# Eleven normalised x pieces turned by DMA transposes instead of by TensorE between products

## The chip, the cores and the metric

The kernel runs on one core of one Trainium2 chip. The metric is the device time of one execution in microseconds (us). Three runs of the kernel before gave 1950.42, 1950.77 and 1952.95 us; the median, 1950.77, is the time before.

## The reference

Eight sequences of 256 tokens and 1024 features pass through cross-attention and a feed-forward block, each with a layer norm ahead of it and a residual behind it:

```
x = x + xattn(layernorm(x), ctx, Wq, bq, Wk, bk)
x = x + ffn(layernorm(x), gate, up, down)

xattn: Q = text @ Wq.T + bq;  K = ctx @ Wk.T + bk
       softmax(Q @ K.T / 32) @ ctx
ffn:   g = x @ Wg.T;  u = x @ Wu.T          (Wg, Wu: 3584 x 1024)
       (silu(g) * u) @ Wd.T                 (Wd: 1024 x 3584)
```

The three feed-forward weights come as 4-bit codes (one int32 each) with a scale for each block of 64, and are decoded in the kernel. Inputs and output are f32.

## The kernel before, in words

**Number format.** Every operand of a large product is split into a high and a low f16 part; a product is three matmuls (high by high, high by low, low by high), so an x form is a pair of f16 tiles.

**Stages.** `prepare` makes the attention matrix and the statistics. `attend` works through the eight batches; `step(b)` on each engine has ten phases. In step b the residual of batch b-1 is added (`residual`), its moments are taken (`moments`), and y of batch b-2 is normalised (`y_normalise`). `feed_forward` follows: 28 stages of seven products by two sides (`slot`), one side being four batches (1024 tokens in f16 forms), and then the down products. ScalarE (ACT) and VectorE (DVE) decode weights all the while, in fixed numbers of steps per phase (`streams.act.run`, `streams.dve.run`), and the SP queue turns the decoded pieces with DMA transposes (`turn_piece`, L301).

**The seven x forms.** The feed-forward products are a seven-product scheme, so a normalised batch gives seven forms j = 0..6 (`t_rows`): three are rows of y (0, 3, 5), four are sums that GpSimd (POOL) makes (`t_sum`; 1, 2, 4, 6). Each form must lie transposed in `T[side][j]` before product j of stage 0 uses it.

**Two ways to turn a form.** The early way (batches 0 to 4, and j = 0, 1, 2 of batch 5; 38 pieces): `t_hi` on ACT and `t_lo` on DVE write the f16 pair into a ring of four slots `t16` (T_RING = 4; `t_hi` waits until the piece four numbers earlier has been turned), `t_turn` on SP issues a DMA transpose into a second ring, `t_store` on SP stores it to the DRAM buffer `keep_x`, and POOL loads all of a form for a side at once (`t_load`, L1254; 1 MB for side 0, 256 or 512 KB for side 1). The late way (`LATE`, 18 pieces: j = 3, 5, 4, 6 of batch 5 and all of batches 6 and 7): `late_turn` issues four 128x128 f32 transposes on TensorE (PE) into a PSUM bank, `late_hi` (ACT, L1273) and `late_lo` (DVE, L1280) write the f16 pair from the bank straight to its place. Late turns 0 to 3 lie in the last attention step, 4 to 17 ahead of the products of stage 0, their number by product written out by hand:

```
then.product(pe, 0); turn_probs(LAST); attended(LAST, 0..3)
m = 4
for k, count in enumerate((2, 2, 2, 1, 0, 2, 2, 1, 1, 1), 1):
    for _ in range(count): ...; late_turn(nc, pe, t, m); m += 1
    then.product(pe, k)
```

**Order around the change.** All engines run in program order. In stage 0, product k is form k of side 0 for k = 0..6 and form k-7 of side 1 for k = 7..13. Product k of side 0 waits for the load `T[0][k]`; on side 1 for the load `T[1][k-7]` and for the late forms. In the handover POOL's order is: the loads of side 0 (j = 0, then 1 to 6), the loads (1, 3), (1, 4), (1, 5), (1, 6), the four sums of batch 6, the loads (1, 0), (1, 1), (1, 2), the four sums of batch 7. `copied` (ACT) and `combined` (DVE) move products between PSUM banks: product 4 waits for `combined(2)`, which DVE runs behind `scales(7)`. The SP queue stores y of batch 6, the last two pieces, y of batch 7 (`store_y`, L1369), and then turns weights. Loads by POOL are on DMA queue q0, everything from SP on q1; both use the same 16 DMA engines.

## Time and profile before

| | before |
|---|---|
| median of three runs | 1950.77 us |
| the profiled execution's own time | 1948.33 us |
| its span, first to last instruction | 1946.5 us |
| PE busy | 1909.0 us (98%) |
| DVE busy | 1621.4 us (83%) |
| ACT busy | 1454.8 us (75%) |
| SP queue and POOL queue, share of the 16 DMA engines | 38.5%, 24.3% |

The span is that of one profiled execution; 1.8 us of its time lie around the span. A group of instructions is named by line, engine, operation and tile. Times in views by time are us from the start of the span. The handover from attention to feed-forward, where the change lies, is at 370 to 440 us.

### The profile page before, as it was taken

The numbers are of one execution on the slowest core, as the hardware profiler recorded it, in microseconds if no ns is written. First come the engines' busy times: TensorE is split into PE (matmuls) and PEld (weight loads), VectorE is DVE, ScalarE is ACT, GpSimd is POOL, SyncE is SP. The second block draws the span as 40 slices with busy tenths as digits, with TensorE's granted clock in tenths as the row PEclk, the third lists the DMA queues.
The fourth block names the chain that finished last, engine by engine and source line by source line (L and its number), as shares of the span: only waits on it lengthen the run. The fifth ranks groups of instructions, "written<-read, shape, count | busy, mean of one in ns | idle before, by whom it ended". The sixth has DMA issues, their size and how long they took to land.

```text
span 1946.5 us, 29468 instructions
## 1 busy us (share of the span) xinstructions
PE 1909.0 (98%) x9758; PEld 969.8 (50%) x9758; DVE 1621.4 (83%) x2671; ACT 1454.8 (75%) x2710; POOL 372.7 (19%) x570
## 2 busy tenths in 40 slices
PE   8989999989999999999999999999999999999999
PEld 3468888744444444444444444444444444444444
DVE  6758899977898898898898898898798888896963
ACT  3867768567989988988988988988999999900000
POOL 0011434431121121121121121121132222200010
PEclk9999999999999999999999999999999999999999
DMA  9123999964555555455455455455488999983462
GB/s 350 31 71 93 211 296 271 270 238 107 130 141 125 125 143 124 127 148 125 121 145 130 121 140 136 119 139 133 115 209 228 242 223 202 246 255 131 161 229 85
DMA packets 427416, 323.00 MB, mean 166 GB/s; under 512 B 361088, under 2 KB 361088, under 8 KB 425344
## 3 DMA queue, kind: packets, MB, share of 16 engines
q1 hardware_dynamic: 381152, 167.47, 38.5%
q0 software_dynamic: 44032, 153.65, 24.3%
q8 instruction: 77, 1.26, 0.3%
q14 instruction: 75, 0.61, 0.1%
q10 hardware_dynamic: 2080, 0.01, 0.1%
HBM read 154.31 MB, written 82.31 MB: 122 GB/s over the span
## 4 chain that ended last, share of the span: by engine, by line
PE 57%; ACT 19%; DVE 8%; issue 7%; DMA 2%; SPq 1%; POOL 1%; DVEq 0%; ACTq 0%; POOLq 0%
PE ps L2108 35%; PE ps L2150 12%; PE ps L1524 7%; ACT sq L346 7%; ACT sq L342 5%; ACT w L346 2%; DVE w L362 2%; ACT w L342 2%; PE ps L1559 1%; PE ps L1497 1%; DVE tail L2260 1%; ACT halves L414 1%; ACT tail L2181 1%; DVE halves L430 1%; ACT tail L2196 1%
## 5 line engine op out<-in xcount | busy, mean ns | idle before, releaser
L2108 PE MATMUL ps<-T,wS 128*128 128x512 f16 x4704 | 1017.6, 379 | 4.3 <-DVE ps L2215 2.7
L2108 PEld LDWEIGHTS ps<-T,wS 128*128 128x128 f16 x4704 | 459.8, 98 | 558.6 <-issue 5.1
L346 ACT ACTIVATE sq<-sq 128x512 f32<-128x512 f32 x898 | 520.0, 635 | 0.0
L362 DVE SCALAR_TENSOR_TENSOR w<-sq,w 128x512 f32<-128x512 f32 x590 | 417.5, 708 | 115.3 <-ACT sq L346 105.5
L342 ACT ACTIVATE sq<-q 128x512 f32<-128x512 int32 x598 | 366.3, 640 | 50.9 <-DVE w L362 46.5
L2150 PE MATMUL ps<-T,tail 128*128 128x512 f16 x1584 | 345.0, 379 | 5.5 <-issue 2.4
L2150 PEld LDWEIGHTS ps<-T,tail 128*128 128x128 f16 x1584 | 154.6, 98 | 193.6 <-issue 5.1
L1524 PE MATMUL ps<-T 128*128 128x256 f16 x1536 | 171.3, 273 | 1.9 <-DVE T L1740 1.9
L2150 PE MATMUL ps<-T,wS 128*128 128x512 f16 x768 | 168.7, 379 | 3.6 <-DMA wS<-keep_h 2.5
L430 DVE SCALAR_TENSOR_TENSOR halves<-w,halves 128x512 f16<-128x512 f32 x240 | 163.9, 692 | 6.8 <-ACT halves L414 6.4
L2056 POOL DMA_DIRECT2D keep_h<-tail x196 | 106.7, 545 | 296.1 <-DVE tail L2260 292.3
L1524 PEld LDWEIGHTS ps<-T 128*128 128x128 f16 x1536 | 150.2, 98 | 19.3 <-DVE T L1740 2.1
L414 ACT CAST halves<-w 128x512 f16<-128x512 f32 x204 | 127.5, 626 | 40.8 <-DVE w L362 31.5
L2260 DVE SCALAR_TENSOR_TENSOR tail<-tail 128x512 f16<-128x512 f32 x196 | 134.1, 684 | 10.6 <-ACT tail L2196 10.5
L2196 ACT CAST tail<-tail 128x512 f16<-128x512 f32 x196 | 120.6, 616 | 5.4 <-DVE tail L2229 5.4
L2150 PEld LDWEIGHTS ps<-T,wS 128*128 128x128 f16 x768 | 74.6, 98 | 95.4 <-issue 4.2
L284 POOL DMA_DIRECT2D q<-in_L_ffn_up_q x52 | 28.1, 540 | 353.5 <-DVE w L362 257.3
L1428 POOL TENSOR_TENSOR T<-tail,T 128x256 f16<-128x256 f32 x64 | 58.7, 917 | 188.5 <-ACT T L1646 188.5
L287 POOL DMA_DIRECT2D q<-in_L_ffn_down_q x56 | 42.9, 766 | 227.7 <-DVE w L362 75.7
L2229 DVE SCALAR_TENSOR_TENSOR tail<-ps,up_out,tail 128x512 f32<-128x512 f32 x112 | 83.6, 747 | 2.1 <-PE ps L2108 1.1
L2181 ACT ACTIVATE tail<-ps,gate_out 128x512 f32<-128x512 f32 x112 | 76.3, 681 | 6.0 <-DVE ps L2219 3.6
L399 DVE TENSOR_TENSOR w<-w 128x512 f32<-128x512 f32 x112 | 77.4, 710 | 1.4
(221 smaller groups left out, 1810.4 us busy)
## 6 DMA issues: line engine op xcount, KB each, us to landing
keep_h<-tail POOLq DMA_DIRECT2D x196, 256.0 KB, 2.5
tail<-keep_h POOLq DMA_DIRECT2D x66, 512.0 KB, 5.0
wS<-keep_h POOLq DMA_DIRECT2D x32, 512.0 KB, 5.5
q<-in_L_ffn_down_q POOLq DMA_DIRECT2D x56, 256.0 KB, 4.5
q<-in_L_ffn_up_q POOLq DMA_DIRECT2D x52, 256.0 KB, 2.9
q<-in_L_ffn_gate_q POOLq DMA_DIRECT2D x48, 256.0 KB, 3.4
keep_x<-T SPq DMA_DIRECT2D x38, 256.0 KB, 4.5
T<-in_x SPq DMA_DIRECT2D x9, 1024.0 KB, 8.1
```

The costliest lines, as they stand in the source:

```text
L342: nc.scalar.activation(place, un.q[:, ring, :], ACT.Square, bias=b, scale=a).then_inc(un.s_act, 1)
L346: nc.scalar.activation(place, place, ACT.Square, bias=b, scale=a).then_inc(un.s_act, 1)
L362: nc.vector.scalar_tensor_tensor(out=out, in0=square_place(un, u, i - 1), scalar=FACTORS[i - 1][1], in1=un.w[:, buf, :], op0=ALU.add, op1= ...
L414: nc.scalar.copy(un.halves[:, z % HALF_RING, 0, :], source_of(un, t, z)).then_inc(un.s_whi, 1)
L430: nc.vector.scalar_tensor_tensor(out=un.halves[:, z % HALF_RING, 1, :], in0=source_of(un, t, z), scalar=1.0, in1=un.halves[:, z % HALF_RIN ...
L1524: last = nc.tensor.matmul(r_bank(o), t.A[:, a, k, o * P:(o + 1) * P], xnT[:, c, k, :], start=k == 0 and j == 0, stop=k == KT - 1 and j == ...
L2056: nc.gpsimd.dma_start(t.hs[form, pair, :, side, :], t.hst[:, n % HST_RING].rearrange("p a d -> p (a d)")).then_inc(s_hst[n % HST_RING], 16)
L2108: last = nc.tensor.matmul(ps[:, bank, :], un.wS[:, z % SLOTS, a, kt, :], t.Tp[side][product][:, :, b, kt, :], start=fresh and n == 0, stop ...
L2150: last = nc.tensor.matmul(ps[:, j, :], h[:, j // PAIRS, a, tok], quad(q, c)[:, b].rearrange("p k d -> p (k d)"), start=fresh and n == 0, s ...
L2181: nc.scalar.activation(t.act_buf[e], ps[:, EVICT_BANK[product] + side, :], ACT.Silu, scale=t.gate_out[:, 2 * pair + row:2 * pair + row + 1 ...
L2196: nc.scalar.copy(t.hst[:, n % HST_RING, 0, :], t.act_buf[2 * FORM_BUF[form] + side]).then_inc(s_hhi, 1)
L2260: nc.vector.scalar_tensor_tensor(out=t.hst[:, n % HST_RING, 1, :], in0=t.act_buf[2 * FORM_BUF[form] + side], scalar=1.0, in1=t.hst[:, n % ...
```

## The change

Eleven of the 18 late pieces (j = 3, 4, 5, 6 of batch 5, and the seven of batch 6) leave `LATE` and become `DIRECT`: ACT and DVE write their f16 pair into the ring `t16` as for the early pieces, and SP issues a DMA transpose (`t_direct`) from the ring straight into `T[1][j]`, without the second ring and the store. On side 1, `slot` waits for these too. Batch 6 is numbered in the order 3, 5, 0, 1, 2, 4, 6. The waits until the places are free go from ACT (`late_places_due`) to SP (`direct_place_due`). The two last stores of the early way, the store of y of batch 7 and the eleven transposes interleave on SP. PE keeps late turns only for batch 7, ahead of products 6 to 10 as before. `y_normalise` of batch 7 now waits until all 49 low parts of batches 0 to 6 are written.

```diff
...
-LATE = tuple((BATCH - 3, j) for j in (3, 5, 4, 6)) + tuple((BATCH - 2, j) for j in (3, 5, 0, 1, 2, 4, 6)) + tuple((BATCH - 1, j) for j in (0, 3, 5, 1, 2, 4, 6))
-LATE_BANKS = (0, 1, 0, 1, 5, 1, 5, 1, 5, 1, 5, 1, 5, 7, 0, 7, 0, 7)
+DIRECT_ORDER = (3, 5, 0, 1, 2, 4, 6)
+DIRECT = tuple((BATCH - 3, j) for j in (3, 4, 5, 6)) + tuple((BATCH - 2, j) for j in DIRECT_ORDER)
+LATE = tuple((BATCH - 1, j) for j in (0, 3, 5, 1, 2, 4, 6))
+LATE_BANKS = (1, 5, 7, 0, 7, 0, 7)
...
 def y_normalise(nc, act, t, b, i):
-    wait(act, t.s_tlo, min(PIECES * b, STORED))
-    wait(act, t.s_tp, sum(row < b for row, _ in LATE))
+    wait(act, t.s_tlo, PIECES * b)
...
+def t_number(b, j):
+    return PIECES * b + (j if b < BATCH - 2 else DIRECT_ORDER.index(j))
 def t_hi(nc, act, t, b, j):
-    n = PIECES * b + j
+    n = t_number(b, j)
...
 def t_lo(nc, dve, t, b, j):
-    n = PIECES * b + j
+    n = t_number(b, j)
...
+def t_direct(nc, sp, t, b, j):
+    n = t_number(b, j)
+    sp.wait_ge(t.s_tlo, n + 1)
+    sp.dma_start(t.Tp[1][j][:, b - PAIRS].rearrange("p a k m -> p (a k) m"), t.t16[:, n % T_RING].rearrange("p a d -> p (a d)"),
+                 transpose=True).then_inc(t.s_tt[n % T_RING], 16)
...
 def t_load(nc, pool, t, side, j):
-    batches = [b for b in range(PAIRS * side, PAIRS * (side + 1)) if (b, j) not in LATE]
+    batches = [b for b in range(PAIRS * side, PAIRS * (side + 1)) if (b, j) not in LATE + DIRECT]
...
+        def direct_place_due(j):
+            if j == 3:
+                sp.wait_ge(t.s_store, 16 * (LAST - 1))
+            if j == 4:
+                sp.wait_ge(s_xn, TB * LAST)
+            if j == 5:
+                sp.wait_ge(s_klo, TB * BATCH)
+            if j == 6:
+                sp.wait_ge(s_att, ATT * LAST)
+            if j == 0:
+                sp.wait_ge(s_att, ATT * BATCH)
+            if j == 1:
+                for n in range(STORED - T_RING, STORED):
+                    t_stored(sp, t, n)
+            if j == 2:
+                sp.wait_ge(t.s_store, 16 * LAST)
+        def direct(b, j):
+            direct_place_due(j)
+            t_direct(nc, sp, t, b, j)
...
+            if b == LAST:
+                direct(c, 3)
+                t_store(nc, sp, t, STORED - 2)
+            if b == LAST:
+                direct(c, 4)
+                t_store(nc, sp, t, STORED - 1)
-        for n in range(STORED - 2, STORED):
-            t_store(nc, sp, t, n)
+        for j in (5, 6):
+            direct(LAST - 2, j)
+        for j in DIRECT_ORDER[:4]:
+            direct(LAST - 1, j)
+        sp.wait_ge(t.s_store, 16 * LAST)
         store_y(LAST)
+        for j in DIRECT_ORDER[4:]:
+            direct(LAST - 1, j)
     def gpsimd(pool):
         def step(b):
...
-            else:
-                late_turn(nc, pe, t, 0)
-            else:
-                late_turn(nc, pe, t, 1)
-            else:
-                late_turn(nc, pe, t, 2)
...
-                        else:
-                            late_turn(nc, pe, t, 3)
...
-        pe.wait_ge(t.s_tpl, 3)
-        m = 4
-        for k, count in enumerate((2, 2, 2, 1, 0, 2, 2, 1, 1, 1), 1):
+        m = 0
+        for k, count in enumerate((0, 0, 0, 0, 0, 2, 2, 1, 1, 1), 1):
-                if m == 13:
+                if m == 2:
-                if m == 14:
+                if m == 3:
...
-        def late_places_due(m):
-            if m == 0:
-                act.wait_ge(t.s_store, 16 * (LAST - 1))
-            if m == 1:
-                act.wait_ge(s_klo, TB * BATCH)
-            if m == 3:
-                act.wait_ge(s_att, ATT * LAST)
-            if m == 6:
-                act.wait_ge(s_att, ATT * BATCH)
-            if m == 7:
-                for n in range(STORED - T_RING, STORED):
-                    t_stored(act, t, n)
-            if m == 8:
-                act.wait_ge(t.s_store, 16 * LAST)
         def turned_probs(b):
...
-                else:
-                    late_places_due(g)
-                    late_hi(nc, act, t, g)
-                if old and (more or g == 0):
+                if old:
-            else:
-                late_places_due(3)
-                late_hi(nc, act, t, 3)
-            if old and more:
+            if old:
...
+        t_hi(nc, act, t, LAST - 2, 6)
-        late_hi(nc, act, t, 4)
-        late_hi(nc, act, t, 5)
+        for j in DIRECT_ORDER[:2]:
+            t_hi(nc, act, t, LAST - 1, j)
-        for m in (6, 7):
-            late_places_due(m)
-            late_hi(nc, act, t, m)
+        for j in DIRECT_ORDER[2:4]:
+            t_hi(nc, act, t, LAST - 1, j)
-        late_places_due(8)
-        for m in (8, 9):
-            late_hi(nc, act, t, m)
+        for j in DIRECT_ORDER[4:6]:
+            t_hi(nc, act, t, LAST - 1, j)
-        late_hi(nc, act, t, 10)
+        t_hi(nc, act, t, LAST - 1, DIRECT_ORDER[6])
-        late_hi(nc, act, t, 11)
-        late_hi(nc, act, t, 12)
+        late_hi(nc, act, t, 0)
+        late_hi(nc, act, t, 1)
-        late_hi(nc, act, t, 13)
-        for m in range(14, 18):
+        late_hi(nc, act, t, 2)
+        for m in range(3, 7):
-            then.copied(act, m - 8)
-            streams.act.run(HIDDEN_PHASE + m - 7)
+            then.copied(act, m + 3)
+            streams.act.run(HIDDEN_PHASE + m + 4)
     def vector(dve):
...
-                    else:
-                        late_lo(nc, dve, t, 0)
-            else:
-                late_lo(nc, dve, t, 1)
...
-                late_lo(nc, dve, t, 2)
-                late_lo(nc, dve, t, 3)
-            if old and more:
+            if old:
-            if old and more:
+            if old:
...
+        t_lo(nc, dve, t, LAST - 2, 5)
+        t_lo(nc, dve, t, LAST - 2, 6)
-        late_lo(nc, dve, t, 4)
-        late_lo(nc, dve, t, 5)
+        for j in DIRECT_ORDER[:2]:
+            t_lo(nc, dve, t, LAST - 1, j)
-        late_lo(nc, dve, t, 6)
-        late_lo(nc, dve, t, 7)
+        for j in DIRECT_ORDER[2:4]:
+            t_lo(nc, dve, t, LAST - 1, j)
-        for m in range(8, 11):
-            late_lo(nc, dve, t, m)
+        for j in DIRECT_ORDER[4:]:
+            t_lo(nc, dve, t, LAST - 1, j)
-        late_lo(nc, dve, t, 11)
-        late_lo(nc, dve, t, 12)
+        late_lo(nc, dve, t, 0)
+        late_lo(nc, dve, t, 1)
-        late_lo(nc, dve, t, 13)
-        for m in range(14, 18):
+        late_lo(nc, dve, t, 2)
+        for m in range(3, 7):
-            then.combined(dve, m - 8)
-            streams.dve.run(HIDDEN_PHASE + m - 7)
+            then.combined(dve, m + 3)
+            streams.dve.run(HIDDEN_PHASE + m + 4)
...
+                for b in (BATCH - 3, BATCH - 2):
+                    if (b, product) in DIRECT:
+                        t_turned(pe, t, t_number(b, product))
```

## Rows read from the trace of the kernel before

**Rows 1.** The page: busy time, share of the span and count of each engine.
```profile
PE 1909.0 (98%) x9758; PEld 969.8 (50%) x9758; DVE 1621.4 (83%) x2671; ACT 1454.8 (75%) x2710; POOL 372.7 (19%) x570
```

**Rows 2.** Waits of PE from 440 us on: total us, times, longest.
```profile
PE ps L2108 <- DVE ps L2215: 2.7, 3, 1.8
PE ps L2150 <- DMA wS<-keep_h: 2.5, 2, 1.5
```

**Rows 3.** Line 1265 on PE, the late turns: duration ns, first and last start.
```profile
L1265 PE MATMUL ps<-ident,tail x72: 272/273/328, 374.0 to 430.4; 128*128 128x128 f32 x72
```

**Rows 4.** Timeline of PE: start us, us, group; products 4 and 5, 7, 9.
```profile
410.73 5.34 PE L2108 MATMUL ps<-T,wS 128*128 128x512 f16 x24
...
421.48 2.75 PE L2108 MATMUL ps<-T,wS 128*128 128x512 f16 x12 [0.85 <-DVE T L1280]
...
427.09 0.60 PE L1265 MATMUL ps<-ident,tail 128*128 128x128 f32 x4
427.53 2.75 PE L2108 MATMUL ps<-T,wS 128*128 128x512 f16 x12
```

**Rows 5.** Waits of PE from 386 to 431 us.
```profile
PE ps L1265 <- POOL tail L1184: 1.0, 1, 1.0
PE ps L2108 <- DVE T L1280: 0.9, 1, 0.9
```

**Rows 6.** Lines 1273 and 1280 (late pair), 1213 and 1220 (early pair): duration ns.
```profile
L1273 ACT CAST T<-ps x18: 565/586/603, 376.2 to 430.8; 128x512 f16<-128x512 f32 x18
L1280 DVE TENSOR_TENSOR T<-ps,T x18: 668/679/693, 376.9 to 431.4; 128x512 f16<-128x512 f32 x18
...
L1213 ACT CAST tail<-tail x3: 613/614/634, 372.5 to 376.7; 128x512 f16<-128x512 f32 x3
L1220 DVE SCALAR_TENSOR_TENSOR tail<-tail x9: 676/683/1502, 341.0 to 382.3; 128x512 f16<-128x512 f32 x9
```

**Rows 7.** Line 301: five DMA transposes of 256 KB, back to back; landing times.
```profile
L301 SPq DMA_TRANSPOSE wS<-halves x5: 1231/1290/1304, 438.6 to 444.2; - x5
DMA to landing us min/median/max: 3.2/3.3/3.3
```

**Rows 8.** Stretches: PE, PEld, DVE, ACT, POOL busy, PEclk, DMA share, GB/s.
```profile
391.00:416.00 25.00, 22.10 (x117) 11.61 (x116) 19.10 (x49) 13.61 (x19) 10.89 (x14) 1.00 1.01 403
417.00:423.00 6.00, 5.15 (x29) 2.71 (x28) 5.97 (x7) 6.00 (x13) 3.18 (x2) 1.00 0.01 3
441.00:445.00 4.00, 4.00 (x20) 1.78 (x19) 3.64 (x6) 3.89 (x8) 0.00 (x0) 1.00 1.00 192
```

**Rows 9.** Line 1254, loads: (1,0) to (1,2); landings of (0,2) and (0,3); of (0,5) and (0,6).
```profile
L1254 POOL DMA_DIRECT2D T<-keep_x x3: 530/530/553, 406.9 to 411.2; - x3
DMA to landing us min/median/max: 7.2/7.4/8.0
...
DMA to landing us min/median/max: 10.1/11.1/12.0
...
DMA to landing us min/median/max: 18.3/19.3/20.3
```

**Rows 10.** Timeline of POOL: loads (0,1) to (1,3) issued together; first sum of batch 6.
```profile
387.76 4.07 POOL L1254 DMA_DIRECT2D T<-keep_x  x7 [7.83 <-DMA T<-tail]
...
401.78 1.29 POOL L1184 TENSOR_TENSOR tail<-tail 128x512 f32<-128x512 f32 x1
```

**Rows 11.** Timeline of DVE: first instruction of `scales(7)`, and `combined(2)`.
```profile
405.11 0.27 DVE L1162 BATCH_NORM_AGGREGATE mv<-stats 128x2 f32<-128x12 f32 x2
...
408.83 0.70 DVE L2215 TENSOR_TENSOR ps<-ps,tail 128x512 f32<-128x512 f32 x1
```

**Rows 12.** Line 1369 at 399.1 us: y of batch 7 (1 MB), to landing.
```profile
DMA to landing us min/median/max: 9.6/9.6/9.6
```

**Rows 13.** Stretches around an idle PE, columns as in rows 8.
```profile
62.20:65.50 3.30, 0.00 (x0) 0.00 (x0) 3.23 (x4) 3.30 (x7) 0.00 (x0) 1.00 0.00 0
66.60:70.00 3.40, 3.40 (x10) 1.16 (x8) 3.40 (x7) 1.32 (x2) 0.00 (x0) 0.50 0.00 0
```

## The prediction

> **What bounds the kernel now.** The page comes first: TensorE (PE) is busy for 98% of the span, and the next engine for 83% [rows 1]. Then the waits of PE behind the handover: from 440 us to the end its two largest groups of waits come to 2.7 and 2.5 us in 1500 us [rows 2]. So PE runs without slack from the end of stage 0 on, and whatever the change shifts in the handover arrives at the end of the kernel one for one. The question is only when the products of stage 0 run, and above all the last of them that waits for something.
>
> The third view is the stretches [rows 8]. From 391 to 416 us the 16 DMA engines are busy at a share of 1.01 and move 403 GB/s; from 417 to 423 they are idle. A full DMA system for 25 us, directly ahead of the use of what it moves, is what the reader is to see: it is POOL's fourteen loads of x forms. In the timeline of PE, product 4 starts at 410.73, product 7 (the first on side 1) at 421.48, product 9 at 427.53 [rows 4]. Load (1,0) is issued at 406.9 and lands 8.0 us later, at 414.9; load (1,2) is issued at 411.2 and lands at 411.2 + 7.2 = 418.4 [rows 9]. So product 7 has a slack of 421.48 - 414.9 = 6.6 us against the DMA system and product 9 one of 427.53 - 418.4 = 9.1 us. Every late form that PE turns costs PE time but no DMA time. The change trades in the other direction.
>
> **What leaves PE.** A late turn is four transposes of 273 ns [rows 3], overlapped: from the turn at 427.09 to the product behind it at 427.53 it is 0.44 us [rows 4]. Eleven: 4.8 us. With them can go a late turn's wait of 1.0 us for POOL; the 0.9 us before product 7 belongs to batch 7's forms, which stay [rows 5]. If nothing else came late, PE would reach product 7 some 4.8 to 5.8 us earlier.
>
> **What ACT and DVE do instead.** The same count of instructions: 11 copies of 614 for 586 ns, 11 low parts of 683 for 679 ns [rows 6], +0.3 us on ACT and nothing on DVE. Neither is PE's bound, and the two f16 writes of batch 5 take the gaps where the late pairs were. I take 0. One thing gets better early on: three of four low parts leave DVE's path ahead of the last softmax (3 x 0.68 = 2 us less, one early low part more), so PE's products of that step run about 1.5 us earlier. That is part of the gain above, not an addition to it.
>
> **What the DMA system gets.** Eleven transposes of 256 KB. Five back to back are issued in (444.2 - 438.6) / 4 = 1.40 us each [rows 7], and while they run the DMA share is 1.00 at 192 GB/s [rows 8]: a transpose takes the whole DMA system for 256 KB / 192 GB/s = 1.37 us. I take 1.40; eleven are 15.4 us. No load or store goes: the eleven pieces were never stored. The alternatives for the price: 0.65 us if it moved like a load (256 KB at the 403 GB/s of rows 8), and 0 if it only filled gaps; but there are none from 391 to 416.
>
> The Trainium skill has a rule on just this: "Advanced Engine Details and Errata", section "X-Bar Transpose (TRN2)", says that a transposing DMA is as fast as a plain one. This trace does not agree (192 against 403 GB/s [rows 8]). By the rule eleven would cost 7.2 us of DMA time, and by the bounds below product 7 would start at about 422, close to where it is.
>
> **Where it lands.** All of it is issued before 420 us, since product 7 needs (6,0), product 8 (6,1), product 9 (6,2). The DMA system was full until 416, so the work moves what is behind it. Load (1,0) at 414.9 with all eleven ahead of it lands at 430.3: product 7 at +8.8 us. With only the seven ahead of it that product 7 itself needs by queue order ((5,3) to (5,6), (6,3), (6,5), (6,0): 9.8 us), and the store of y of batch 7 (1 MB, 2.6 us at 403 GB/s), which SP now issues behind (6,1), moved behind it: 414.9 + 9.8 - 2.6 = 422.1, or +0.6. These are the two ends. Which? The two queues share: the 1 MB store issued at 399.1 took 9.6 us [rows 12], and of the loads beside it (the seven of rows 10 are issued 0.58 us apart) (0,3) landed at 388.9 + 12.0 = 400.9 and (0,5) at 390.1 + 18.3 = 408.4 [rows 9, 10]: 7.5 us for 2 MB that 403 GB/s moves in 5.2. So SP's queue gets a good part of the engines when both have work, by my estimate half, and everything issued by 418 us on SP is mostly through by 429: I let ten of the eleven go ahead, 414.9 + 14.0 = 428.9, product 7 at +7.4. Product 9 then has load (1,2) at 418.4 + 14.0 = 432.4, before 428.9 + 2 x 2.6 + 0.9 = 435.0: it runs on, and PE keeps +7.4.
>
> On arbitration the Trainium skill ("DMA: Bandwidth & Descriptors", section "Queues, rings and completion order") says that each DMA engine goes round between the queues that have work, a packet at a time. The store beside the load agrees; how a queue of small transpose packets fares beside packets of 8 KB no row here shows.
>
> **The waits that the change adds, and who stands behind them.** (a) `t_hi` of piece n on ACT waits until n-4 is turned; behind it stand ACT's copies of products. Each generation costs a transpose's landing: 3.3 us alone [rows 7], more when DMA is full. (b) POOL's issues come with the landings: the load (1,6) and then the first sum of batch 6 (401.78 [rows 10]) follow the landing of load (0,3), 388.9 + 12.0 = 400.9 [rows 9]. Five transposes through by then (7.0 us at most) put this sum at up to 408.8. DVE's order is low part of (6,1), `scales(7)` (3.7 us, 405.11 to 408.83), `combined(2)` (0.7) [rows 11], then on PE product 4, before at 410.73 [rows 4]. With the sum at 408.8: 1.3 (sum), 0.6 and 0.7 (pair), 3.7 and 0.7 give 415.8, product 4 at +5.1. That is inside the +7.4 and not added to it. (c) `y_normalise` of batch 7 waits for the low part of (6,6), and through the ring for (6,0); about as late as product 6 and again inside. (d) Product 7 to 13 wait for the transposes themselves; the last is issued by about 418 and landed before product 13. (e) SP's weight turns come behind all this; they are for stage 1, which begins over 20 us after the last x transpose is issued, so I take 0.
>
> **Clock.** After PE was idle from 62.2 to 65.5 the granted clock was 0.50 (1.2 of 2.4 GHz) for 3.4 us [rows 13], which is 1.7 us of work lost. The waits that I expect are of 2 to 4 us each, so there may be one such fall. I leave it out of the sum and in the range.
>
> **The sum.** The profiled execution took 1948.33 us; the change gives 1955.7. The median of the runs shown stands 2.4 us above that execution, so the median after is 1950.8 + 7.4 = 1958.2.
>
> **The rivals.** *A, the gain arrives.* The transposes run in spare DMA time: 1950.8 less 4.8 to 5.8, about 1945.5. For it: PE is the bound and loses 44 instructions. Against it: a share of 1.01 for 25 us, and by the lower of my two ends the load (1,0) alone forbids it. 0.08. *B, it cancels.* Loads go first or a transpose beside loads costs nearer 0.65 us, and product 7 moves by +0.6 to +3.9: about 1953. For it: it is the floor of the DMA sum, PE arrives early and takes each load as it lands. 0.20. *C, the ring locks.* The transposes get nearly nothing beside the loads' 8 KB packets: (5,5) and (5,6) are turned only when the queue of loads is empty (load (0,6), issued at 390.7, lands 20.3 us later at 411.0 [rows 9], and four loads of 256 KB behind it take 2.6 us), plus four transposes of 1.4, 419.2; then pair, scales and `combined(2)` as in (b), 5.7 us: product 4 at 424.9, +14.2, without a fall of the clock: 1965. It decides from the point where a transpose beside loads takes over some 10 us. For it: that order of events leaves the loads on time. Against it: the store's half share [rows 12]. 0.12. *The forecast*, product 7 held by load (1,0) at +4.6 to +8.8, with up to 3 us of clock and gaps: 0.60, own range 1955 to 1962.
>
> **The range and the chances.** 1951 to 1967 takes in the main case, nearly all of B and most of C. A measurement here tells 0.2%, 3.9 us, from no change. Slower by more: 0.60 + 0.12 = 0.72; within: 0.20; faster: 0.08.
>
> **What would show it.** Right: the share stays near 1.0 from 391 to about 430 us; loads (0,3) and (1,0) land at 406 to 409 and 427 to 430; PE waits for DMA `T<-keep_x` ahead of products 2 to 7; product 7 starts near 429 and PE's waits behind 440 are as before. Wrong: product 7 before 421, landings of transposes at 3.3 us in this stretch, or loads landing as before with ACT waiting for `T<-tail` (that is C). The forecast falls if a transpose beside loads takes clearly less than 1.4 us of DMA time, or if what is lost in stage 0 is not still lost at the end.

## The result, and the profile after

The changed kernel takes 1969.15 us (median of four runs, 1966.97 to 1969.76). The kernel before, run beside it, takes 1951.86 us (1950.42 to 1956.26). The ratio is 1.0085 with a 95% interval of 1.007 to 1.01: slower by 17.3 us. The forecast was 1958.2 us with a range of 1951 to 1967. The sign was right, the time lies above the range, and the events are in the main those of rival C.

The profiled execution took 1969.76 us. Its page, busy time by engine, against [rows 1]:

```profile
PE 1910.0 (97%) x9714; PEld 966.2 (49%) x9714; DVE 1616.7 (82%) x2671; ACT 1453.0 (74%) x2710; POOL 371.3 (19%) x570
```

PE has 44 instructions less, the eleven late turns, and is still busy 1.0 us longer; two groups of its matmuls ran at half clock (below). The span grew from 1946.5 to 1967.9 us, so PE's idle time grew by 20.4 us. The waits of PE from 360 to 470 us (us in total, times, longest) show three quarters of it in one row, of a kind that [rows 5] does not have:

```profile
PE ps L2122 <- DVE ps L2229: 15.9, 1, 15.9
```

L2122 are the products, L2229 is `combined(2)` on DVE. The timeline of PE (start us, us, group) gives the place, against [rows 4]:

```profile
395.99 7.93 PE L2122 MATMUL ps<-T,wS 128*128 128x512 f16 x36
419.77 6.95 PE L2122 MATMUL ps<-T,wS 128*128 128x512 f16 x24 [15.85 <-DVE ps L2229]
...
431.61 2.75 PE L2122 MATMUL ps<-T,wS 128*128 128x512 f16 x12
```

Products 1, 2 and 3 run in one go without turns between them; then PE stands for 15.85 us ahead of product 4. Product 7 starts at 431.61 (before 421.48).

From PE the chain is followed backwards, engine by engine. DVE's timeline, where `combined(2)` started at 408.83 before [rows 11]:

```profile
409.41 0.69 DVE L1226 SCALAR_TENSOR_TENSOR tail<-tail 128x512 f16<-128x512 f32 x1 [12.40 <-ACT tail L1219]
...
418.93 0.70 DVE L2229 TENSOR_TENSOR ps<-ps,tail 128x512 f32<-128x512 f32 x1
```

DVE waited 12.40 us for ACT's high part (L1219) of the first form of batch 6. ACT's waits from 385 to 431 us, and its timeline there:

```profile
ACT tail L1219 <- DMA T<-tail: 22.7, 5, 13.9
```

```profile
408.76 0.62 ACT L1219 CAST tail<-tail 128x512 f16<-128x512 f32 x1 [13.93 <-DMA T<-tail]
411.53 0.62 ACT L1219 CAST tail<-tail 128x512 f16<-128x512 f32 x1 [2.15 <-DMA T<-tail]
...
421.76 0.62 ACT L1219 CAST tail<-tail 128x512 f16<-128x512 f32 x1 [5.82 <-DMA T<-tail]
```

The three high parts are those of (6,3), (6,5) and (6,4). This is the ring of four: `t_hi` of a piece waits until the piece four numbers earlier has been turned. Line 1242, the eleven direct transposes, and the first of them alone:

```profile
L1242 SPq DMA_TRANSPOSE T<-tail x11: 1243/2069/18457, 385.8 to 426.7; - x11
...
DMA to landing us min/median/max: 3.2/5.3/23.7
...
DMA to landing us min/median/max: 22.9/22.9/22.9
```

The first, form (5,3), is issued at 385.80 and lands 22.9 us later, at 408.7: that is the 408.76 at which ACT goes on. Alone a transpose lands in 3.3 us [rows 7]. The timeline of the SP queue shows a second effect:

```profile
385.80 1.24 SPq L1242 DMA_TRANSPOSE T<-tail  x1
387.08 0.57 SPq L1254 DMA_DIRECT2D keep_x<-T  x1
387.75 18.46 SPq L1242 DMA_TRANSPOSE T<-tail  x1
406.26 0.93 SPq L1254 DMA_DIRECT2D keep_x<-T  x1
407.29 14.28 SPq L1242 DMA_TRANSPOSE T<-tail  x6
```

The instruction that issues the second transpose occupies SP for 18.46 us. Whatever is behind it in SP's program, here the store at 406.26, is not issued before.

Why does 256 KB take 22.9 us? The DMA view of 391 to 403 us (packets, MB, share of the 16 engines) answers it:

```profile
DMA packets 1213, 4.62 MB, mean 385 GB/s; under 512 B 669, under 2 KB 669, under 8 KB 669
...
q0 software_dynamic: 606, 4.44, 96.8%
q1 hardware_dynamic: 605, 0.15, 7.0%
```

POOL's loads (q0) and SP's transposes (q1) send the same number of packets, 606 and 605. But 605 packets of q1 carry 0.15 MB, 256 B each, and most of those of q0 carry 8 KB. A transpose is 256 KB / 256 B = 1024 packets; at 605 in 12 us that is 20.3 us, by estimate. The landing is made up a little differently: from 388 to 390 us q1 sends 1 packet, from 390 to 404 it sends 701 beside 714 of q0, and from 404 to 408.7 another 417 beside 416 (the store and the next transpose among them), faster because the packets of the later loads are smaller (416 of them carry 1.47 MB). Why nothing of the transpose moves in the first 4 us, no run shows. Once the loads have run dry, from 411 to 414 us, q1 alone sends 2782 packets in 3 us:

```profile
q1 hardware_dynamic: 2782, 0.87, 119.5%
```

The Trainium skill says on "DMA: Bandwidth & Descriptors", section "Queues, rings and completion order", that each DMA engine goes round between its queues at the granularity of a packet. The trace agrees, 606 to 605; whether a packet of the profile is what that page calls a packet, no run shows, and the counts would agree either way. What follows from it is that a queue's share of the bytes is set by its packet size.

The loads hardly notice. Load (0,3) is issued at 386.3 and lands 10.6 us later, at 396.9 (before 12.0 us later, at 400.9), and the first sum of batch 6 starts on POOL at 397.78 (before 401.78 [rows 10]). The stretches (PE, PEld, DVE, ACT, POOL busy, PEclk, DMA share, GB/s), against [rows 8]:

```profile
391.00:416.00 25.00, 12.92 (x57) 5.55 (x55) 8.63 (x20) 6.48 (x9) 8.16 (x10) 0.77 1.05 344
406.10:423.00 16.90, 3.23 (x8) 1.20 (x9) 8.91 (x25) 5.33 (x9) 1.05 (x2) 0.50 1.09 277
388.90:392.30 3.40, 2.98 (x8) 1.05 (x9) 2.98 (x16) 0.63 (x2) 0.88 (x2) 0.51 1.01 375
```

In the second and third the granted clock is 0.50 and 0.51, the lower level, after PE had been idle from 403.9 and for most of 385.1 to 389.3. Products 4 and 5 took 6.95 us for 5.34 (1.6 us), the 24 matmuls of L1543 at 389.32 took 6.83 for 5.34 at 371.70 (1.5 us).

**The account.** Of every kernel below the medians stand first, then the starts of products 0, 4 and 10 in its profiled execution. "0 to 10" is how much longer it takes from product 0 to product 10 than before (43.7 us), called the stretch 0 to 10 from here on; behind product 10 the shift stays constant to the end of the hidden stages (+11.4 at 442 us, +11.2 at 1435 in the changed kernel). The start of product 0 differs by execution, 382.3 to 387.5, which is why the stretch is compared and not the start of product 10. The ratios given with the experiments come from the comparison with the runs beside them and are not the quotients of these medians.

```
kernel            median   before   difference   product 0      4     10   0 to 10
before                                               386.8  410.7  430.6
after            1969.15  1951.86     +17.3          382.3  419.8  442.0   +15.9
e1_after_2k      1979.95  1951.88     +28.1          385.2  441.0  462.3   +33.5
e2_before_2k     1977.40  1951.88     +25.5          385.1  437.5  457.4   +28.7
e3_after_plain   1957.99  1951.88      +6.1          386.8  418.8  439.3    +8.7
e4_before_delay  1961.99  1951.88     +10.1          385.1  409.0  439.0   +10.2
e5_batch5        1967.26  1951.22     +16.0          385.8  425.7  445.7   +16.1
e6_before_double 1951.54  1951.22      +0.3          387.5  411.8  431.6    +0.4
e7_after_order   1967.87  1951.22     +16.7          385.5  409.4  448.4   +19.1
e8_after_queue   1954.54  1951.22      +3.3          386.2  413.9  435.0    +5.2
e9_batch5_last   1952.40  1952.34      +0.1          384.8  411.2  431.0    +2.5
e10_batch5_first 1951.61  1952.34      -0.7          385.7  414.5  434.5    +5.0
```

### The profile page after: what moved, and what is told of

It reads as the page before. It is cut to its first block, busy times and chain, and to the rows that moved or that the text cites. A ratio compares the mean times of both kernels' runs of the same rounds, so it can differ in the third digit from the quotient of the medians.

```text
span 1967.9 us, 29402 instructions
## 1 busy us (share of the span) xinstructions
PE 1910.0 (97%) x9714; PEld 966.2 (49%) x9714; DVE 1616.7 (82%) x2671; ACT 1453.0 (74%) x2710; POOL 371.3 (19%) x570
## 4 chain that ended last, share of the span: by engine, by line
PE 62%; ACT 18%; DVE 6%; issue 4%; DMA 2%; SPq 1%; DVEq 0%; ACTq 0%; POOLq 0%
PE ps L2122 38%; PE ps L2164 12%; PE ps L1570 9%; ACT sq L348 6%; ACT sq L344 5%; ACT w L348 2%; PE ps L1599 2%; PE ps L1543 2%; ACT w L344 2%; DVE w L364 1%; SPq L1242 1%; DMA T<-halves 1%; ACT halves L416 1%; DVE tail L2274 1%; ACT tail L2195 1%
## 5 line engine op out<-in xcount | busy, mean ns | idle before, releaser
L2122 PE MATMUL ps<-T,wS 128*128 128x512 f16 x4704 | 1018.9, 379 | 19.1 <-DVE ps L2229 18.4
L2122 PEld LDWEIGHTS ps<-T,wS 128*128 128x128 f16 x4704 | 460.1, 98 | 575.7 <-issue 22.3
L2274 DVE SCALAR_TENSOR_TENSOR tail<-tail 128x512 f16<-128x512 f32 x196 | 133.9, 683 | 10.4 <-ACT tail L2210 10.2
```

Of the source, the lines that this page charges most:

```text
L2122: last = nc.tensor.matmul(ps[:, bank, :], un.wS[:, z % SLOTS, a, kt, :], t.Tp[side][product][:, :, b, kt, :], start=fresh and n == 0, stop ...
L2274: nc.vector.scalar_tensor_tensor(out=t.hst[:, n % HST_RING, 1, :], in0=t.act_buf[2 * FORM_BUF[form] + side], scalar=1.0, in1=t.hst[:, n % ...
```

## The experiments

The theory is that beside 8 KB packets a transpose gets one packet of 256 B for each of theirs, and that the ring and the order of SP's program turn its late landing into a wait of PE. The rivals were that transposing itself is slow whatever stands beside it, that the order on DVE and ACT makes the wait, that the loss arises behind the handover, and that all of it is the plain DMA work of the forecast.

**e1: the changed kernel with loads of 2 KB rows.** The DRAM buffer is laid out by batch ahead of partition, so a load's rows are 2 KB; its store and its load are indexed to match.

```diff
-    args.append(nc.dram_tensor("keep_x", (PIECES, P, BATCH, 2 * BANK), F16).ap())
+    args.append(nc.dram_tensor("keep_x", (PIECES, BATCH, P, 2 * BANK), F16).ap())
...
```

> The changed kernel with one edit: the DRAM buffer keep_x has the batch ahead of the partition, so that a load of an x form reads rows of 2 KB in place of rows of 8 KB. Same instructions, same bytes. Theory P (packets): beside the loads the transposes go forward one 256-byte packet for each packet of a load. With packets a quarter as long the first transpose, 22.9 us in the changed kernel, lands in 5 to 8 us, PE's wait of 15.9 us before product 4 shrinks to under 4 us, product 7 starts near 420 to 424 instead of 431.6, and the kernel is 8 to 12 us faster than the changed one: about 1958. Theory W (work): the eleven transposes cost DMA time (15.4 us) whatever stands beside them; nothing changes, 1969.

The median is 1979.95 us, ratio 1.0146 (1.0103 to 1.0188). The landings became short, but the time grew, and PE's wait ahead of product 4 grew with it, to 22.6 us where under 4 was expected. Line 1242, the waits of POOL from 370 to 450 us, and its queue from 391 to 403 us:

```profile
L1242 SPq DMA_TRANSPOSE T<-tail x11: 1232/1288/4613, 388.6 to 447.5; - x11
...
DMA to landing us min/median/max: 3.1/7.0/8.4
```

```profile
POOL T L1268 <- issue: 37.5, 6, 8.4
```

```profile
q0 software_dynamic: 455, 1.80, 43.5%
```

No transpose takes over 8.4 us now. But POOL, which issued seven loads in 4.07 us before [rows 10], issues the loads of side 0 one at a time with waits of up to 8.4 us, and the sums of batch 6, behind the loads in its program, start at 432.68. The short landings are therefore weak evidence for the packets: 455 packets carry 1.80 MB, 4 KB each and not 2, and they take only 43.5% of the engines' time. Where both queues have work the counts are again about equal (92 to 83 from 393 to 394 us), but from 396 to 400 us q1 sends 2513 packets with no load beside them. The edit brought a second cost, which e2 measures.

**e2: the kernel before with the same layout.** The same diff.

> The kernel before with the same buffer layout (2 KB rows) and nothing else: the control for the run above. Both theories: within 2 us of before, 1950 to 1953, since no transpose runs beside the loads there and loads have 3 to 9 us of slack. Were the loads much slower in 2 KB rows, product 1 or 2 would wait for them and this kernel would be 3 us or more slower.

1977.4 us, ratio 1.0144 (1.01 to 1.0188), where no difference was expected. The waits of POOL, of PE from 370 to 450 us, and POOL's in the kernel before:

```profile
POOL T L1254 <- issue: 34.3, 6, 7.5
```

```profile
PE ps L1265 <- POOL tail L1184: 26.0, 1, 26.0
```

```profile
POOL T L1254 <- issue: 11.6, 5, 4.3
```

There is no transpose of the change in it and the loss is 25.5 us. So all that e1 loses, but for 2.6 us, can be the loads' issuing, and e1 says nothing on the time of the change. That the number of rows is what fills POOL's queue is inferred: one load with four times the rows stands where several stood.

**e3: the eleven as plain copies.** They move the same 256 KB in 128 rows of 2 KB; the eleven forms are not transposed.

```diff
-    sp.dma_start(t.Tp[1][j][:, b - PAIRS].rearrange("p a k m -> p (a k) m"), ..., transpose=True)...
+    sp.dma_start(t.Tp[1][j][:, b - PAIRS].rearrange("p a k m -> p (a k m)"), ...)...
```

> The changed kernel with the eleven transposing DMAs turned into plain copies of the same 256 KB (rows of 2 KB) into the same places; the eleven forms are then not transposed. Same waits, same queue, same bytes. Theory P: such a copy has 8 packets per engine in place of 64, so beside the loads it takes 3 to 5 us, ACT does not stand at the ring, and the handover costs less than before: PE gains its 4.8 us, 1946 to 1950. Theory W: the copies still take 11 x 0.65 = 7.2 us of DMA time, so loads land later and the time is 1950 to 1954. If the locking had another cause (the ring, the order on SP), it would stay at 1965 to 1969.

1957.99 us, ratio 1.0032 (1.0014 to 1.0051): 11.2 us of the 17.3 go, and 6.1 stay where a gain was expected. Line 1242 and PE's wait:

```profile
L1242 SPq DMA_DIRECT2D T<-tail x11: 464/465/543, 390.3 to 421.9; - x11
...
DMA to landing us min/median/max: 4.6/8.8/19.6
```

```profile
PE ps L2122 <- DVE ps L2229: 10.2, 1, 10.2
```

and the packets from 395 to 411 us, while both queues have work:

```profile
q0 software_dynamic: 746, 5.28, 79.1%
q1 hardware_dynamic: 746, 1.37, 22.2%
```

It is the same lock, smaller. The two queues send packet for packet, 746 to 746, and with packets of 2 KB q1 carries 1.37 MB in 16 us where the transposes carried 0.15 in 12. A copy is 128 packets where a transpose is 1024; but up to four copies and two stores are queued behind one another, and the slowest still lands after 19.6 us. Issuing takes 0.47 us each, so it no longer holds SP. By this reading it is the number of packets queued in all that counts, not that of one copy; no run varies it by itself.

**e4: the kernel before with PE held up ahead of product 7.** 52 additional clears of a PSUM bank and no DMA.

```diff
         if k == FIRST_SLOTS:
-            clear(pe, Y + 1)
+            for _ in range(1 + 52):
+                clear(pe, Y + 1)
```

> The kernel before with PE held up by hand: 52 extra matmuls into the free bank Y+1 ahead of product 7 (52 x 0.216 = 11.2 us), which is about what the change costs in stage 0 (+11.4 us at product 10). The output is the same. It asks where the other 10 us of the changed kernel come from, which appear in the down products. Theory D1: they follow from the shift alone (the decode and its DMAs meet at other moments): then this kernel too shows 5 us or more in the down products, about 1967 in all. Theory D2: they belong to the change or to the single execution: then the down products start and end shifted by the same 11.2 us, about 1962.

PE is held for 11.60 us:

```profile
418.53 11.60 PE L2114 MATMUL ps<-T,wS 128*128 128x512 f16 x53
```

The stretch 0 to 10 grew by 10.2 us and the median by 10.1 (ratio 1.005, 1.0024 to 1.0076). A shift in the handover arrives one for one. In the down products single executions wander: this one ended at +4.1, the changed kernel's went from +11.2 to +21.8, and runs of one kernel lie up to 19 us apart (1950.62 to 1969.68 in this one). A profile's end is therefore no measure here; the stretch and the median are.

**e5: only batch 5's four forms directly.** Batch 6 stays with PE's late turns; `DIRECT` holds four pieces, `LATE` fourteen. Against the kernel before:

```diff
+DIRECT = tuple((BATCH - 3, j) for j in (3, 4, 5, 6))
+LATE = tuple((BATCH - 2, j) for j in (3, 5, 0, 1, 2, 4, 6)) + tuple((BATCH - 1, j) for j in (0, 3, 5, 1, 2, 4, 6))
...
+            if b == LAST:
+                direct(3)
+                t_store(nc, sp, t, STORED - 2)
...
+            if b == LAST:
+                direct(4)
+                t_store(nc, sp, t, STORED - 1)
...
+        for j in (5, 6):
+            direct(j)
         store_y(LAST)
```

> Part of the change alone: only the four forms of batch 5 are turned by DMAs straight into their places, and all seven of batch 6 stay with PE (14 late turns). The ring of four slots is then not written again behind (5,3) to (5,6), so no engine waits for these transposes before products 10 to 13. Theory P (packets, and the ring that locks): the four transposes again land 20 us or more after their issue, but nobody stands at them; PE keeps 4 x 0.44 = 1.8 us and product 4 is not late: 1948 to 1951, 1 to 3 us faster than before. Theory W (DMA work): four transposes put 5.6 us before load (1,0), inside its slack of 6.6 us: the same 1949 to 1951. If instead the time is 3 us or more above before, the harm does not need the ring.

1967.26 us, ratio 1.0076 (1.0051 to 1.01): four transposes lose nearly what eleven lose, where no loss was expected. The expectation looked at ACT's ring, which no form of batch 6 uses here. SP's timeline, and the waits of ACT and of PE:

```profile
391.60 17.94 SPq L1237 DMA_TRANSPOSE T<-tail  x1
409.58 0.93 SPq L1249 DMA_DIRECT2D keep_x<-T  x1
```

```profile
418.46 0.58 ACT L1282 CAST T<-ps 128x512 f16<-128x512 f32 x1 [15.71 <-DMA keep_x<-T]
```

```profile
PE ps L1274 <- DVE T L1289: 12.9, 1, 12.9
```

The store of the last stored piece stands on SP behind the second transpose, is issued at 409.58 and lands 8.7 us later. ACT's late high parts of batch 6 need their places free, and wait for that store (`late_places_due`); product 3 comes 13.7 us late. So there are two ways from a slow transpose to PE: the ring, and what SP has queued behind it. In the changed kernel both are there.

**e6: the kernel before with the eleven late turns done twice.** How much is PE's time in these turns worth?

```diff
-    for k in range(4):
+    for k in (0, 1, 2, 3) * (2 if m < 11 else 1):
```

> The kernel before with the eleven late turns in question done twice on PE (44 more f32 transposes, same result). It prices what the change takes off PE. If a late turn costs 0.44 us on the path that sets the end, the handover grows by 11 x 0.44 = 4.8 us and the kernel takes 1955.5 to 1957; if part of it lies under waits for other engines, less: 3 us.

1951.54 us, ratio 1.0015 (0.9991 to 1.0039). The interval reaches from 1.8 us less to 7.6 us more, so the median does not decide on 4.8 us. The stretch 0 to 10 grew by 0.4 us; only seven of the eleven turns lie in it, 3.1 us of added work. The waits of PE from 380 to 450 us; in the kernel before there are also 1.2 us for L1612 and 0.7 for L1280, and 1.0 where 0.3 stands:

```profile
PE ps L1497 <- DVE tail L1769: 1.5, 1, 1.5
PE ps L2108 <- DVE T L1280: 0.9, 1, 0.9
PE ps L1265 <- POOL tail L1184: 0.3, 1, 0.3
```

The wait of 1.2 us for ACT (L1612, the last softmax) is gone here. Counted from the 24 matmuls of L1497 behind it (392.89 before, 392.21 here) to product 10, the same 3.1 us cost 1.8. So part of the additional work fills time in which PE would have waited. Adding is not removing, but these waits are there in the kernel before, so the gain to be had from PE was under 4.8 us; how far under, one execution does not tell. That PE is busy for 98% of the whole span says nothing on this stretch.

What removing brings can be seen for the four turns ahead of product 0. The wait for the last softmax, in the kernel before and in e9 (in the changed kernel, L1522, it is the same 2.2 us):

```profile
PE ps L1476 <- ACT tail L1612: 1.2, 1, 1.2
```

```profile
PE ps L1498 <- ACT tail L1625: 2.2, 1, 2.2
```

Of the 1.8 us that the four turns cost PE, 1.0 comes back as a longer wait.

**e7: the changed kernel with the critical work first.** `copied(1)` goes ahead of ACT's high parts of batch 6; moments, scales and `combined(2)` go ahead of DVE's low parts.

```diff
...
         moments(LAST)
-        for j in DIRECT_ORDER[2:4]:
-            t_lo(nc, dve, t, LAST - 1, j)
         scales(LAST)
         then.combined(dve, 2)
-        for j in DIRECT_ORDER[4:]:
+        for j in DIRECT_ORDER:
             t_lo(nc, dve, t, LAST - 1, j)
```

> The changed kernel with the same work in another order on two engines: ACT copies product 1 ahead of the first batch 6 forms, and DVE runs the moments and scales of batch 7 and combined(2) ahead of all low parts of batch 6. Nothing that product 4 or 5 needs then stands behind a wait for a transpose. Theory P: products 4 and 5 run on, but y_normalise of batch 7 still waits for the low part of (6,6) and through the ring for the transpose of (6,0), which starts only when the loads are through; the wait of PE moves in front of product 6 and ends about 5 us earlier: product 7 near 426 in place of 431.6, time 1962 to 1966. If the cause were the order alone (ACT and DVE standing in front of product 4 and nothing else), all of the loss would go: 1948 to 1953.

1967.87 us, ratio 1.0082 (1.0052 to 1.0112). The wait went from product 4 (409.4, 10.4 us earlier) to the turn ahead of product 6, as expected in place but not in size:

```profile
PE ps L1279 <- ACT tail L1176: 15.7, 1, 15.7
```

L1176 is `y_normalise` of batch 7, which needs all low parts of batch 6, and these go through the ring. Order on the engines decides only which instruction shows the wait.

**e8: the loads in SP's queue too, in an order written by hand.** With one queue there is no turn-taking between two.

```diff
+        load(0, 1)
+        direct(LAST - 2, 5)
+        direct(LAST - 2, 6)
+        load(0, 2, 3)
+        direct(LAST - 1, 3)
+        direct(LAST - 1, 5)
+        load(0, 4)
...
+        load(0, 6)
+        load(1, 3, 4, 5, 6, 0)
+        direct(LAST - 1, 2)
```

> The changed kernel with the thirteen later loads of x forms issued by SP instead of POOL, in one queue with the eleven transposes and in an order written by hand in which products need them; POOL makes only sums. In one queue a transpose is not alternated packet by packet with a load. Same DMA work. Theory P with W as its floor: transposes land in 4 to 9 us, the wait of 15.9 us before product 4 is gone, and what stays is DMA work: product 7 waits for load (1,0), at 423 to 427, product 9 likewise; 1953 to 1957, 12 us or more faster than the changed kernel and still not faster than before. If the transposes were slow for another reason (their places, the ring, ACT), it would stay near 1965 to 1969.

1954.54 us, ratio 1.0009 (0.9988 to 1.0031), as expected: +3.3 us against the kernel before, where the changed kernel has +17.3. Line 1242, PE's largest waits and the stretch:

```profile
DMA to landing us min/median/max: 3.3/6.4/8.3
```

```profile
PE ps L2116 <- issue: 5.2, 3, 2.5
```

```profile
391.00:416.00 25.00, 19.03 (x74) 7.88 (x75) 18.11 (x48) 10.38 (x16) 5.90 (x4) 0.86 1.11 304
```

All eleven transposes, the same bytes; none takes over 8.3 us and the lock is gone. Hence it was not transposing as such, nor the ring, nor the places. The run changes the queue and the order on it together, and no run has the one without the other; that the turn-taking is what the order by hand avoids rests on the packet counts. What stays is 5.2 us in the stretch 0 to 10. Of these, 3.0 are half clock: the 24 matmuls of L1537 took 6.68 us for 5.35, products 2 and 3 took 7.03 for 5.34, and the granted clock from 391 to 416 is 0.86. 25 us of a full DMA system move 304 GB/s instead of 403: the transposes' work is real, as the forecast had it, but small beside the lock.

**e9 and e10: e5 with another order on SP.** In e9 both stores and the store of y of batch 7 go first and the four transposes last. In e10 the two stores go first, then the transposes, then the store of y.

```diff
-        for j in (5, 6):
-            direct(j)
+        for n in range(STORED - 2, STORED):
+            t_store(nc, sp, t, n)
         store_y(LAST)
+        for j in (3, 4, 5, 6):
+            direct(j)
```

> As the batch 5 run (four forms by DMA, fourteen late turns), with one move on SP: the last two stores of the early way and the store of y of batch 7 are issued first, the four transposes behind them. In the batch 5 run ACT waited for those two stores, which stood on SP behind a transpose that took 26 us. Theory P (a transpose alternates packet by packet with the loads, and the cost is what stands behind it): nothing that is needed before product 10 now stands behind a transpose; the transposes run when the loads are nearly through and land by 425. The 15 us of the batch 5 run are gone: 1948 to 1952, 0 to 2 us faster than before. If the direct transposes did harm in another way than by what stands behind them, it would stay above 1955.

> The same with the two stores first, then the four transposes, then the store of y of batch 7. The transposes again start beside the loads and land 15 to 25 us after their issue, but only the store of y of batch 7 stands behind them, which the silu of product 8 and its place wait for. Theory P: landing times as in the batch 5 run and still no loss, 1948 to 1953. If slow transposes by themselves cost time, it would be slower than the run with the transposes last by 5 us or more.

1952.4 us (ratio 0.9999, 0.9978 to 1.0021) and 1951.61 us (1.0001, 0.9981 to 1.0021): the 16.0 us of e5 are gone. The SP queue of e10 and its line 1237:

```profile
389.18 35.24 SPq L1237 DMA_TRANSPOSE T<-tail  x4
424.48 0.58 SPq L1389 DMA_DIRECT2D keep_y<-tail  x1
```

```profile
DMA to landing us min/median/max: 10.6/22.9/36.0
```

These transposes are slower than those of e5 (5.6/15.6/26.0), and the kernel is 16 us faster. A slow transpose costs little by itself while what needs it is far off; it costs through what stands behind it. These two leave the time as it was, to within the 4 us that the intervals allow; the stretches 0 to 10, +2.5 and +5.0 us in one execution each, leave room for a small loss. No version here beats the kernel before, and four turns less on PE gave nothing that could be measured.

Beside the longer wait shown with e6 there is a second reason. The 24 matmuls behind that wait, in e9:

```profile
391.80 8.02 PE L1519 MATMUL ps<-T,tail 128*128 128x512 f16 x24 [1.42 <-DVE tail L1776]
```

The kernel before takes 5.35 us for them at full clock. Here they take 2.7 us more, and the granted clock from 390 to 400 us is 0.66 (before 1.00); that is all of e9's +2.5. In e10 they take 7.04 us, and product 2, behind a wait of 2.2 us for POOL, takes 4.44 for 2.75. Of the eight executions profiled without the four early turns seven show this fall (all but e5), of the four with them one (e2). Ahead of these matmuls PE is idle for about 2.2 and 1.4 us in those eight, and for 1.2 and 1.5 in the kernel before. So work taken off PE ahead of a wait left PE idle for longer, and most often the clock fell behind it.

## Why the prediction was wrong

1. *PE bounds the kernel and a shift in the handover arrives one for one*: right. +11.4 us at 442 and +11.2 at 1435 in one execution; 10.2 in the stretch 0 to 10 and 10.1 in the median in e4.
2. *What leaves PE, 4.8 us*: right in size ([rows 3], 44 instructions) and wrong in worth. "If nothing else came late, PE would reach product 7 some 4.8 to 5.8 us earlier" did not ask what PE waits for between the turns. The four turns ahead of product 0 gave back 1.0 of 1.8 us as a longer wait, and in seven of eight executions more than the rest as half clock; the seven behind it were worth at most about 1.8 of 3.1 us by e6, if adding tells of removing. Rival A lost its ground with this too.
3. *What the DMA system gets, eleven times 1.40*: the work is there. The stretch from 391 to 416 us moves 344 GB/s at a share of 1.05, where before 403 [rows 8]. It is not what PE waited for: no row of PE's waits names `T<-keep_x`.
4. *Where it lands: "SP's queue gets a good part of the engines when both have work, by my estimate half", and from that ten of eleven ahead of load (1,0)*: **this step failed.** It came from a 1 MB store that took 9.6 us beside the loads [rows 12]. For that store it was true. In the kernel before, from 403 to 407 us, while it moves, the two queues sent

```profile
q1 hardware_dynamic: 110, 0.90, 53.1%
q0 software_dynamic: 111, 0.79, 47.1%
```

   packet for packet, and because both send packets of about 8 KB, that is half the engines. (In the first 3.5 us after its issue no packet of the store moved.) A transpose sends 256 B each. [Rows 8] do not show that; the DMA view of 441 to 445 us, 3085 packets for 0.77 MB, does, and I had not set the two side by side. So the transposes got 7.0% of the time and 0.15 of 4.6 MB, not half, and the loads came on time (396.9 us for (0,3), not 406 to 409).
5. *The added waits (a) to (e), put inside the +7.4*: the places were right, all sizes fell with step 4. (a) was priced at "3.3 us alone [rows 7], more when DMA is full": the first landing took 22.9 us and ACT waited 13.9 for it; it is what (b) then carries to product 4. (c) shows in e7 as 15.7 us. (e), what stands on SP behind a transpose, I took as 0 because stage 1 is far; the stores behind it were not looked at, and e5 shows that they alone cost 16 us.
6. *Clock, in the range and not in the sum*: 1.6 and 1.5 us at half clock, the first behind the wait ahead of product 4, the second behind the longer wait for the last softmax. One such fall was allowed for, and two came.
7. *Rival C*, at 0.12, had the mechanism and 1965 us. It put product 4 at 424.9 without a fall of the clock, and it came at 419.8; from product 0, which came 4.5 us early in this execution, it is +13.5 against the +14.2 of C. Then products 4 and 5 at half clock (1.6 us) and a turn for which PE waited 0.27 us bring most of the rest up to 15.9. That SP itself stands behind a transpose is not in C. Its point of decision, "a transpose beside loads takes over some 10 us", was the right question.

What stays open: the 0 to 5 us between the stretch 0 to 10 and the median in the table, which lie within the spread of single executions; how the 2.2 us of e8 that are not half clock split between DMA work and an order written by hand; and how far the order of e8 alone, without the change of queue, would have gone.

## What to carry to other kernels

Before a transfer is put beside another queue's transfers, count packets, not bytes: size / packet size over the rate at which the other queue's packets go. Then list what its issuing engine has queued behind it and who waits for that; a ring of few slots, or a store behind a transfer that can't be issued, turns a slow landing into a wait of the bound engine. And where work is to be taken off the busiest engine, look first at what that engine waits for just behind the work, and double the work: if doubling costs less than the work itself, taking it away will hardly bring all of it.

## What the runs showed of the hardware that I had not expected

- Where both DMA queues had work they sent packet for packet, whatever the size: 606 to 605 with 8 KB against 256 B, 746 to 746 with 8 KB against 2 KB (e3), 111 to 110 with 8 KB against 8 KB (before). A transposing DMA of 256 KB is 1024 packets; it landed in 3.3 us alone and in 22.9 us beside loads. The Trainium skill, "Advanced Engine Details and Errata", section "X-Bar Transpose (TRN2)", holds transposing DMAs to be as fast as plain ones. These runs do not agree: 192 GB/s alone where loads move 403 [rows 8], and beside loads 0.15 MB in 12 us where plain copies and stores move 1.37 MB in 16 (e3).
- The instruction that issues a transpose can occupy SP's queue for 18.46 us (four of them 35.24 us in e10), while a plain copy in the same place takes 0.47 us (e3).
- Behind a wait for the last softmax of 2.2 us the granted clock fell to the lower level in seven of eight executions, behind one of at most 1.3 us in one of four, and the next 24 matmuls took up to 8.21 us (e1) instead of 5.35.
- Loads with rows of 2 KB instead of 8 KB, the same bytes in packets of 4 KB, lengthen POOL's waits to issue from 11.6 to 34.3 us and cost a kernel 25.5 us (e2).
